# Splitting the query and key products out of a score buffer, over three engines

## What is computed

```python
h = _layernorm(x) * (1 + ca) + sa
qkv = h @ W_qkv.T + b_qkv                  # layer 1: wq, wk, wv without a bias
q, k, v = qkv[0], qkv[1], qkv[2]
scores = einsum('bhqd,bhkd->bhqk', q, k) / sqrt(Hd)      # layer 1: / sqrt(128)
probs = softmax(scores + bias)             # bias -slope * |i - j| in layer 0 alone
out = einsum('bhqk,bhkd->bhqd', probs, v)
```

## Time and profile before

| what | value |
|---|---|
| device time, median of 3 runs | 2230.93 us (2229.56 to 2236.93) |
| the profiled execution | 2240.09 us, of which the span of its instructions is 2238.3 us |
| busy in the span | PE 1715.6 us (77%), DVE 1638.5 (73%), ACT 992.4 (44%), POOL 884.0 (39%) |
| mean granted TensorE clock | 0.935 of full speed |

### The profile page before, as it was taken

How to read it: one execution, slowest core, us unless ns; L and a number is a source line. 1 busy time by engine, 2 the same in 40 slices (tenths; PEclk the granted TensorE clock), 3 DMA queues, 4 the chain that set the end, 5 groups by cost and what they waited for, 6 DMA issues and landing times. The chain is left out here.

```text
span 2238.3 us, 53972 instructions
## 1 busy us (share of the span) xinstructions
PE 1715.6 (77%) x14370; PEld 1185.4 (53%) x14370; DVE 1638.5 (73%) x5605; ACT 992.4 (44%) x1839; POOL 884.0 (39%) x932
## 2 busy tenths in 40 slices
PE   2588888888888838999935777777877777719997
PEld 1355555555555527989822444444444444417775
DVE  3478888888888845667626888888888888624453
ACT  0265555655555522222212555555555555503322
POOL 0224444444444333444423444444444444203343
PEclk9899999999999968999966999999999999959999
DMA  4334434443434322222235445555455454243332
GB/s 139 49 65 73 69 70 75 70 73 68 74 69 71 64 61 65 67 67 67 66 130 89 91 97 108 102 101 111 96 101 113 94 101 102 56 147 93 93 93 63
DMA packets 267153, 190.44 MB, mean 85 GB/s; under 512 B 26080, under 2 KB 257282, under 8 KB 266326
## 3 DMA queue, kind: packets, MB, share of 16 engines
q1 hardware_dynamic: 251738, 154.75, 35.2%
q0 software_dynamic: 15360, 35.03, 5.3%
HBM read 94.68 MB, written 53.18 MB: 66 GB/s over the span
## 5 line engine op out<-in xcount | busy, mean ns | idle before, releaser
L873 DVE TENSOR_REDUCE mx<-A 128x2 f32<-128x512 f32 x1024 | 685.8, 681 | 147.3 <-PE A L1123 116.1
L728 ACT ACTIVATE probs<-B 128x1024 f32<-128x1024 f32 x512 | 524.4, 1024 | 401.9 <-PE B L1143 211.3
L1123 PE MATMUL A<-stack 126*128 126x256 bf16 x2048 | 397.0, 283 | 168.6 <-DVE mx L873 112.0
L1143 PE MATMUL B<-stack 128*128 128x256 bf16 x2048 | 364.3, 281 | 40.6 <-DMA stack<-mrow 39.2
L1123 PEld LDWEIGHTS A<-stack 126*128 126x128 bf16 x2048 | 159.7, 99 | 343.2 <-DVE mx L873 259.7
L1161 PE MATMUL M<-probs,vals 128*32 128x256 f32 x4096 | 292.8, 404 | 26.5 <-DVE On L896 22.8
L1143 PEld LDWEIGHTS B<-stack 128*128 128x128 bf16 x2048 | 198.5, 102 | 97.7 <-ACT probs L728 26.8
L637 POOL DMA_INDIRECT gathered<-h,slot_in x192 | 187.7, 978 | 155.2 <-DVE slot_in L1017 109.6
L624 POOL TENSOR_TENSOR h<-xn,back_rows 128x256 f32<-128x256 f32 x64 | 46.4, 726 | 487.0 <-DVE xn L828 487.0
L1563 PE MATMUL A<-w2s,hid 128*128 128x128 f32 x1792 | 230.4, 278 | 9.0 <-issue 9.0
L1563 PEld LDWEIGHTS A<-w2s,hid 128*128 128x128 f32 x1792 | 211.8, 192 | 18.4 <-issue 13.4
(11 more groups left out here) (190 smaller groups left out, 2720.6 us busy)
## 6 DMA issues: line engine op xcount, KB each, us to landing
stack<-parts SPq DMA_DIRECT2D x768, 64.0 KB
xt<-gathered SPq DMA_DIRECT2D x112, 132.0 KB, 2.2
probs<-gathered SPq DMA_DIRECT2D x40, 256.0 KB, 2.7
w<-in_w SPq DMA_DIRECT2D x4, 2048.0 KB
back_rows<-mod_rows SPq DMA_DIRECT2D x64, 128.0 KB, 3.4
x_mid<-X SPq DMA_DIRECT2D x64, 128.0 KB, 2.1
Y<-expert_out SPq DMA_DIRECT2D x64, 128.0 KB
X<-in_x SPq DMA_DIRECT2D x32, 128.0 KB, 3.0
```

The costliest lines, as they stand in the source:

```text
L728: act.activation(probs[c % 4][:, :, :, :], Bp[c % 2][:, :, :, :], ACT.Exp, scale=EXP_SCALE[l][c // 4]).then_inc(b_exp.handle, 1)
L873: dve.tensor_reduce(mx[u][:, h, :], A[h % 2][:, :, :], AX.X, ALU.max).then_inc(a_max.handle, 1)
L1123: ins = pe.matmul(A[h % 2][:, t, :], stack[u][0:n, h, 0, t * P:(t + 1) * P], stack[u][0:n, h, 1, :], start=True, stop=True)
L1143: ins = pe.matmul(Bp[c % 2][:, j, t, :], stack[u][:, h, 1, t * P:(t + 1) * P], stack[u][:, h, 0, :], start=True, stop=(l == 1))
```

## The change

`project_qk` writes to the first bank of `Bp[0]` instead of `M0`, and the products stay there. ACT reads them once for the high part (`high_part`, with the bias added in layer 0), DVE reads them once more and subtracts the high part (`remainder`, two instructions in layer 0, one in layer 1), ACT casts the remainder to the middle part (`mid_part`), and POOL makes the low part alone (`low_part`). The scale of the queries is multiplied into `wq` once, at the start. Since `Bp[0]` is taken from `project_qk` until `remainder` is done, chunks 1, 2, 3, 5 and 7 go to `Bp[1]` and chunks 0, 4 and 6 to `Bp[0]`. The waits of the other users of `M0` are adapted. Left out below are the declarations of names and semaphores.

```diff
+                ch.mark(dve.tensor_tensor(wq[:, :, :], wq[:, :, :], scale_row[:, :, :], ALU.mult))
...
+BUFFER = (0, 1, 1, 1, 0, 1, 0, 1)
+HOLD = 4
...
-            def split_qk(b, k, u):
...
-                pool.wait_ge(qk_f32.handle, qk_f32.after(b))
-
-                for half in range(2):
-                    pool.wait_ge(stack_in[u][half], stack_in.of(k - 1))
-                p = parts[u]
-                one = ones_col[:, :, :].broadcast_to([P, 2, S])
-                ch.link(pool.tensor_tensor(p[:, :, 0, :], qk[:, :, :], one, ALU.mult))
-                ch.link(pool.tensor_tensor(rem[:, :, :], qk[:, :, :], p[:, :, 0, :], ALU.subtract))
-                ch.link(pool.tensor_tensor(p[:, :, 1, :], rem[:, :, :], one, ALU.mult))
-                pool.tensor_tensor(p[:, :, 2, :], rem[:, :, :], p[:, :, 1, :], ALU.subtract).then_inc(split.handle, 1)
+            def low_part(b, k, u):
+                pool.wait_ge(qk_mid.handle, qk_mid.after(b))
+                pool.tensor_tensor(parts[u][:, :, 2, :], rem[:, :, :], parts[u][:, :, 1, :], ALU.subtract)\
+                    .then_inc(split.handle, 1)
...
-                    split_qk(*at(1))
+                    low_part(*at(1))
...
-            def read_qk(b, k, u):
+            def high_part(b, k, u):
                 act.wait_ge(qk_proj.handle, qk_proj.after(b))
-                act.wait_ge(split.handle, split.after(b - 1))
-                m = M0[:, :].rearrange("p (j s) -> p j s", j=2)
+                for half in range(2):
+                    act.wait_ge(stack_in[u][half], stack_in.of(k - 1))
+                src, dst = Bp[0][:, 0, :, :], parts[u][:, :, 0, :]
                 if l:
-                    ch.mark(act.activation(qk[:, 0, :], m[:, 0, :], ACT.Identity, scale=q_scale[:, 1:2]))
-                    ins = act.activation(qk[:, 1, :], m[:, 1, :], ACT.Copy)
+                    ins = act.activation(dst, src, ACT.Copy)
                 else:
-                    ch.mark(act.activation(qk[:, 0, :], m[:, 0, :], ACT.Identity, bias=qs_bias[:, 0:1],
-                                           scale=q_scale[:, 0:1]))
-                    ins = act.activation(qk[:, 1, :], m[:, 1, :], ACT.Identity, bias=qk_bias[:, 1:2])
-                ins.then_inc(qk_f32.handle, 1)
+                    ch.mark(act.activation(dst[:, 0, :], src[:, 0, :], ACT.Identity, bias=qs_bias[:, 0:1]))
+                    ins = act.activation(dst[:, 1, :], src[:, 1, :], ACT.Identity, bias=qk_bias[:, 1:2])
+                ins.then_inc(qk_high.handle, 1)
+
+            def mid_part(b, k, u):
+                act.wait_ge(qk_rem.handle, qk_rem.after(b))
+                act.activation(parts[u][:, :, 1, :], rem[:, :, :], ACT.Copy).then_inc(qk_mid.handle, 1)
...
-                act.activation(probs[c % 4][:, :, :, :], Bp[c % 2][:, :, :, :], ACT.Exp,
+                act.activation(probs[c % 4][:, :, :, :], Bp[BUFFER[c]][:, :, :, :], ACT.Exp,
...
                 chunk(1)
-                step(read_qk, 1)
+                step(high_part, 1)
                 chunk(2)
                 layer(1, first_rsqrt, 2)
                 step(max_rows, -1, 1)
+                step(mid_part, 1)
                 chunk(3)
...
+            def remainder(b, k, u):
+                dve.wait_ge(qk_high.handle, qk_high.after(b))
+                dve.wait_ge(split.handle, split.after(b - 1))
+                src, high = Bp[0][:, 0, :, :], parts[u][:, :, 0, :]
+                if l:
+                    ins = dve.tensor_tensor(rem[:, :, :], src, high, ALU.subtract)
+                else:
+                    ch.mark(dve.scalar_tensor_tensor(out=rem[:, 0, :], in0=src[:, 0, :], scalar=qs_bias[:, 0:1],
+                                                     in1=high[:, 0, :], op0=ALU.add, op1=ALU.subtract))
+                    ins = dve.scalar_tensor_tensor(out=rem[:, 1, :], in0=src[:, 1, :], scalar=qk_bias[:, 1:2],
+                                                   in1=high[:, 1, :], op0=ALU.add, op1=ALU.subtract)
+                ins.then_inc(qk_rem.handle, 1)
...
                 maxima(6, 1)
+                step(remainder, 1)
                 layer(0, choose_first, -3)
...
             def project_qk(b, k, u):
+
                 pe.wait_ge(h_ready.handle, h_ready.after(b))
-                pe.matmul(M0[:, 0:S], wq[:, l, :], hT[u][:, :], start=True, stop=True)
-                pe.matmul(M0[:, S:2 * S], wk[:, l, :], hT[u][:, :], start=True, stop=True).then_inc(qk_proj.handle, 1)
+                pe.wait_ge(qk_rem.handle, qk_rem.after(b - 1))
+                pe.wait_ge(b_exp.handle, b_exp.after(b - 2, 1))
+                pe.matmul(Bp[0][:, 0, 0, :], wq[:, l, :], hT[u][:, :], start=True, stop=True)
+                pe.matmul(Bp[0][:, 0, 1, :], wk[:, l, :], hT[u][:, :], start=True, stop=True).then_inc(qk_proj.handle, 1)
...
-            def scores_b(b, k, u, c):
...
-                pe.wait_ge(b_exp.handle, b_exp.after(b, c - 1) if c >= 2 else b_exp.after(b - 1, HH + c - 1))
+                if c == HOLD:
+                    if hold is None:
+                        pe.wait_ge(b_exp.handle, b_exp.after(b, 1))
+                    else:
+                        pe.wait_ge(qk_rem.handle, qk_rem.after(hold))
+                else:
+                    last = [d for d in range(c) if BUFFER[d] == BUFFER[c]]
+                    pe.wait_ge(b_exp.handle, b_exp.after(b, last[-1] + 1) if last else b_exp.after(b - 1, HH + c - 1))
...
-                        ins = pe.matmul(Bp[c % 2][:, j, t, :], stack[u][:, h, 1, t * P:(t + 1) * P],
+                        ins = pe.matmul(Bp[BUFFER[c]][:, j, t, :], stack[u][:, h, 1, t * P:(t + 1) * P],
...
-                        scores_b(*at(-1), c)
+                        scores_b(*at(-1), c, at(1)[0] if at(1) else None)
...
                 chunk(1)
                 if at(1):
-                    m0_read((h2T_read, -3))
                     project_qk(*at(1))
                 a_pass(4)
                 heads_step(turn_heads, -2, 1)
                 a_pass(5)
                 if at(-3):
-                    m0_read((qk_f32, 1))
                     gate(*at(-3))
                 chunk(2)
                 a_pass(6)
                 if at(-1):
-                    m0_read((logits_read, -3), (qk_f32, 1))
+                    m0_read((logits_read, -3), (h_ready, 1), (mT_read, -1, 1))
                     turn_max(*at(-1), 1)
...
                 if at(0):
-                    m0_read((mT_read, -1, 2), (qk_f32, 1))
+                    m0_read((mT_read, -1, 2), (h_ready, 1))
...
-                    m0_read((mT_read, 0, 1), (qk_f32, 1))
+                    m0_read((mT_read, 0, 1), (h_ready, 1))
...
+        "q_scale": q_scale, "scale_row": np.broadcast_to(q_scale.T[None], (P, 2, P)).copy(),
```

More of the change, by code:

```diff
@@ L44 @@
 EPS_IN = 1e-6
-DVE_MARKS = (34, 39)
+DVE_MARKS = (35, 39)
 MIDST = (2, 4, 5, 7, 8, 10, 11, 13, 14)
@@ L154, in build @@
         ident_b = sb("ident_b", [P, P], BF16)
+        scale_row = sb("scale_row", [P, 2, P])
         slope_ident = sb("slope_ident", [P, HH, P], BF16)
@@ L195, in build @@
         hT = [sb(f"hT{u}", [P, S]) for u in range(2)]
-        qk = sb("qk", [P, 2, S])
+        qk = sb("qk", [P, 2, D])
         rem = sb("rem", [P, 2, S])
@@ L265, in build @@
         loads = [
-            (ident[:, :], a["ident"]), (ident_b[:, :], a["ident_b"].bitcast(BF16)), (slope_ident[:, :, :], a["slope_ident"].bitcast(BF16)),
+            (ident[:, :], a["ident"]), (ident_b[:, :], a["ident_b"].bitcast(BF16)),
+            (scale_row[:, :, :], a["scale_row"]), (slope_ident[:, :, :], a["slope_ident"].bitcast(BF16)),
             (dist[:, :], a["dist"].bitcast(BF16)), (before_tri[:, :], a["before_tri"].bitcast(BF16)), (ones_b[:, :], a["ones_b"].bitcast(BF16)),
@@ L411, in attention @@
 def attention(nc, l, g):
-    (X, XR, X1, st, mv, rs, xn, hT, qk, rem, parts, stack, vals, mx, mneg, mrow, probs, heads, rsum, On, OnT, yT,
+    (X, XR, X1, st, mv, rs, xn, hT, rem, parts, stack, vals, mx, mneg, mrow, probs, heads, rsum, On, OnT, yT,
      st2, mv2, rs2, xn2, front_rows, back_rows, xb, qs_bias, h2, h3, h2T, eps_col, lg, rt, r1, sel, slot_in, token_ids, run) = (g[n] for n in (
-        "X XR X1 st mv rs xn hT qk rem parts stack vals mx mneg mrow probs heads rsum On OnT yT "
+        "X XR X1 st mv rs xn hT rem parts stack vals mx mneg mrow probs heads rsum On OnT yT "
         "st2 mv2 rs2 xn2 front_rows back_rows xb qs_bias h2 h3 h2T eps_col lg rt r1 sel slot_in token_ids run").split())
@@ L454, in attention @@
     y_view = expert_out[0][0:2 * B * S, :].rearrange("(c b t p) d -> c b p t d", c=2, b=B, p=P)
-    stats, xn_ready, qk_f32, x1_ready, stats2, xn2_ready, logits_read, slots_ready, pos_read = signals(
-        "stats", "xn_ready", "qk_f32", "x1_ready", "stats2", "xn2_ready", "logits_read", "slots_ready", "pos_read")
+    stats, xn_ready, x1_ready, stats2, xn2_ready, logits_read, slots_ready, pos_read = signals(
```

(20 more changed lines are left out.)

2 lines of the change are left out of this document (1 added, 1 removed).

## The result

The changed kernel takes 2307.8 us (median; 2296.9 to 2318.0) where the kernel before, on the same chip, takes 2230.2: a ratio of 1.033, interval 1.031 to 1.036. It is slower by 78 us; the forecast was 18 us faster, and 2307.8 lies far outside its range. The profiled execution after took 2318.0 us, against 2240.1 before.

What follows compares the result with a forecast made beforehand. DVE, busy 88% of both attention stages, was taken to set the ticks. Terms -17 - 3 + 3 - 2 + 1 = -18 us, carried to the median: 2230.9 - 18 = 2213 us, range 2190 to 2238.

Steps and rivals of the forecast that it cites:

- +0.1, bounds -0.24 and +0.40: Layer 1, us per tick: L919 loses its hold, `remainder` is added, L828's pair stays held; +3 us over 28 ticks.
- if PE's clock falls oftener in layer 1: Named as a way for the prediction to be wrong: PE's lower clock level more often; no change there was priced.
- -0.62 a tick: Layer 0's sum per tick in us: -0.45 - 1.55 + 0.78 + 0.6; -17 us over 28 ticks.
- -3 for late ticks: Layer 0: PE's 0.66 us wait for ACT ahead of `project_qk`, in 5 of 27 ticks, ends; -3 us.
- the 0.45 taken for `gate`: Layer 0, per tick: `gate` no longer waits for a copy out of `M0`, saving 0.45 us ahead of the seventh maximum.
- step 2: Layer 0: three of four POOL instructions go, and with them DVE's holds on L881, L961, L959, L958; 1.55 us per tick.
- step 4: Layer 0: POOL's low part can hold one DVE instruction, L961 for 0.95 us or `split_max` for 0.15; 0.6 taken.
- rival B: The hold stays: POOL first in every tick, L961 held 0.95; layer 0 -0.27 a tick; 2226 us; chance 0.20.
- the list of signs: What would show each step, including L919 falling to 0.43 us and the L828 pair staying near 0.59 each.
- The earlier stack lets PE wait there instead: Layer 0: PE's 23.8 us of stack waits should vanish, but chunk 0 would wait for row maxima's transfer; no gain.
- Rival C: Slower, ACT trapped: late `mid_part` delays `values`, closing a ring from DVE over ACT and PE; +17, 2248 us; chance 0.13.
- Rival A: The hold clears: POOL later than L961 in every tick; layer 0 -1.07 a tick; 2197 us; chance 0.20.

Runs made afterwards that it cites:

- the 10 instructions: The changed kernel with 10 VectorE instructions added ahead of layer 1, each only adding 1 to a semaphore nobody reads: 2213.3 us, ratio 0.991.
- the kernel before with 18 instructions: The kernel before with 18 VectorE instructions that do nothing added ahead of layer 1: 2233.9 us, ratio 1.000.
- the reordered kernel: The changed kernel with 10 do-nothing instructions, VectorE's order changed so the remainder comes later and the low part runs beside maxima: 2327.3 us, ratio 1.043.
- the runs with the middle part later: The changed kernel with 10 do-nothing instructions, plus the middle part cast twice (2217.2 us), or cast behind `values` in layer 0 with `gate_values` ahead of `low_part` in layer 1 (2188.9).

## Why the prediction was wrong

The step that failed is layer 1's, "+0.1, bounds -0.24 and +0.40", times 28: it was to be +3 us with -7 to +11, and was +102.8 in 26 ticks. All its pieces were durations of instructions and holds. None was for DVE getting the instructions. The change moved layer 1's loop by 36 records, into a third stretch of code, and each return then met two standstills: 71.4 us of standing still, 26.0 more of waiting for PE, whose clock fell to its lower level oftener (a granted clock of 0.84 over the stage, against 0.91 with the 10 instructions and 0.94 before). The last sentence had named that as a way to be wrong, "if PE's clock falls oftener in layer 1"; the fall is there, but it follows from the standstill. What could have been seen: the 12 waits on "issue" before, 4.0 us, mark the returns of a loop of 278 records, and 36 more ahead of it could be counted from the diff, roughly. What could not: the border's place, which no row of before shows.

With the code's place put right, by ten instructions that compute nothing, the kernel takes 2213.3 us, and the sum's 2213 can be held against it term by term. Against the kernel before on the same chip, 2233.9, that is 20.6 us faster, for a forecast of 18. That it comes so close is in part luck: the ticks of layer 0 gave some 15 us and not 20, and layer 1 and the rest of the program, which were to cost 2, gave back the difference and more.

- Layer 0: with -0.62 a tick and -3 for late ticks, -20 in 28; measured -15.9 in 27 (-14.4 with the 10 instructions). DVE's idle time for PE's scores fell from 28.9 us to 15.3, or 0.50 a tick against the 0.45 taken for `gate`. The holds of L881, L959 and L958 went, as in step 2. `remainder` costs 0.78 from start to start (it starts at 405.12 and 405.51, and `choose_first` at 405.90, in the tick shown above), the value taken.
- The size that was off is step 4, "so I take the middle, 0.6": POOL was first in 27 ticks of 27, 0.75 us after the remainder's end, near the short end of 0.72 to 0.87, and the hold was the 0.95 of rival B. Two hand-over times seen in layer 1 were no ground for a mean in layer 0, where one order of events came in each tick. Rival B's time did not follow: with the -3 for late ticks it had -0.38 a tick for layer 0, and -0.53 to -0.59 were measured. The last 0.15 to 0.2 is mostly in three groups that step 2 had not listed: L972 fell from 215 to 159 ns, L983 from 196 to 166 and L880 from 230 to 217, with the 10 instructions 3.0 us in all or 0.11 a tick; 0.05 more is the idle time for PE, 0.50 for 0.45.
- Layer 1, with the 10 instructions: L919 (L938 there) fell from 1267 to 426 ns, the remainder took 681, as the step had it. The pair of L828 rose from 591 to 817, where the list of signs had it stay near 590:

```profile
L834 DVE TENSOR_SCALAR xn<-X,mv,rs 128x128 f32<-128x128 f32 x52 | 40.4, 817 | 0.0
...
L880 DVE TENSOR_TENSOR rem<-B,parts 128x512 f32<-128x512 f32 x26 | 17.7, 681 | 0.0
...
L938 DVE TENSOR_TENSOR h<-On,xb 128x256 f32<-128x256 f32 x26 | 11.1, 426 | 0.6
```

  The 26 ticks took 1.9 us less than before, -0.07 a tick against +0.1. That is no difference that can be told: the kernel before with 18 instructions took 621.0 us for them, 3.5 more than without.
- "The earlier stack lets PE wait there instead", for the row maxima's transfer, was wrong in layer 0: PE's 23.8 us of waits for the stack went, and the wait for the transfer came to 1.1 in all.
- Rival C had the right side, slower, by a mechanism that did not act: its ring exists, as the reordered kernel shows, but had room in the changed one.
- Rival A did not come about; the runs with the middle part later show what it was worth: 9.7 us in layer 0 with the cast written twice, 13.1 with it behind `values`.

## What to carry to other kernels

When a change adds or removes instructions on an engine with a long loop, count where the loop comes to lie, not only what the instructions take: here six instructions that do nothing, ahead of the loop, were worth 102 us, five times the change. The signs are idle time on "issue" at the loop's return, as often as the loop goes back, and more packets on the instruction queue. And before a forecast is given up, take such a side effect away and measure again: here the sum for the work itself then came within 3 us, with some of its terms off both ways.

## What the runs showed of the hardware

The border lies between the 7th and the 8th instruction of the changed kernel's loop. In the kernel before, counted by the same records, a loop that starts 25 ahead of it and ends 253 behind it is not fetched anew, and one that starts 17 ahead and ends 261 behind it is: so, by this count, the stretches are between 253 and 261 instructions long, and two of them are kept. The Trainium skill, "Advanced Engine Details and Errata", section "ISA Cache", has 256 instructions to a line and two lines; the runs agree. The Trainium skill, "Runtime: NRT & Kernel Launch", section "Instruction fetch mechanics", has it that a taken branch to code outside the two pages waits for a transfer. In the five kernels here that show it, the wait is 2.6 to 3.4 us at each return. Some 3 to 4 more come at the border with 3 or 7 instructions ahead of it, and none with 14 or 17. What each of the about 5 packets to a return holds was not followed up.

What PE does meanwhile, changed kernel, in steps of 2 us from 1506 (the first number behind DVE, ACT and POOL is the granted clock):

```profile
1506.00:1508.00 2.00, 0.00 (x0) 0.00 (x0) 0.00 (x0) 0.00 (x0) 0.55 (x1) 0.94 0.63 78
1508.00:1510.00 2.00, 0.00 (x0) 0.00 (x0) 0.18 (x1) 0.00 (x0) 0.00 (x0) 0.50 0.49 51
1510.00:1512.00 2.00, 1.43 (x14) 0.57 (x18) 1.80 (x3) 0.00 (x0) 0.00 (x0) 0.50 0.03 7
1512.00:1514.00 2.00, 2.00 (x17) 1.00 (x10) 0.00 (x0) 0.68 (x2) 0.00 (x0) 0.50 0.00 0
1514.00:1516.00 2.00, 2.00 (x14) 1.59 (x13) 1.13 (x4) 1.31 (x3) 0.00 (x0) 0.86 0.00 0
```

PE is idle from 1506 to 1510, its clock is at the lower level, 0.50, from 1508 to 1514, and DVE, which caused it, waits in its turn from 1512 to 1514. So standstills of 71 us came to cost over 100. How much of the 26.0 us more of waiting is the clock's, and how much PE's own late start, was not separated; from 1502 to 1504, ahead of the standstill, the clock was at 0.50 too.

A hold can also fall on an instruction with one input in SBUF: `split_max`'s first, 128 x 16 from float32 to bf16, took 465 ns on the mean of both in a tick with the low part beside one of them, and 217 with the low part earlier. The held one is held whole: in one tick the low part runs from 148.31 to 149.47, and the instruction from 148.84 to 149.50.
